# Weight low parts ahead of the output weight's, ten small products in four groups, and the low rank's rows in another bank

## The reference, cut to what matters

```python
x = x + L0_xattn(layernorm(x), ctx, mask, position_bias, ...)   # 32 heads of 128
x = x + L0_ffn(layernorm(x), W_base, lora_A, lora_B, router_W, router_b, prior, active)
x = x + L1_xattn(layernorm(x), ctx, Wq, bq, Wk, bk)             # one head of 512
x = x + L1_ffn(layernorm(x), dequantised 6-bit weights, bias)
```

```python
y = einsum('bth,oh->bto', x, W_base) + b_base
A, Bm = lora_A[active], lora_B[active]
z = einsum('bth,erh->bter', x, A)
contribs = einsum('bter,eor->bteo', z, Bm) * 2.0
logits = (einsum('bth,eh->bte', x, router_W) + router_b)[..., active]
alpha = softmax(log(prior[active] + 1e-12) + logits)
return y + einsum('bteo,bte->bto', contribs, alpha)
```

## Time and profile before

| | |
|---|---|
| median of 3 runs | 953.75 us (952.48 to 953.95) |
| the profiled execution | 953.5 us, of which the span is 951.6 us |
| mean granted TensorE clock | 0.996 of full |
| PE busy | 935.6 us, 98% of the span |
| PE weight loads busy | 816.3 us, 86% |
| DVE busy | 633.0 us, 67% |
| ACT busy | 409.0 us, 43% |
| POOL busy | 522.7 us, 55% |

### The profile page before, as it was taken

How to read it: one execution, slowest core, us unless ns; L and a number is a source line. 1 busy time by engine, 2 the same in 40 slices (tenths; PEclk the granted TensorE clock), 3 DMA queues, 4 the chain that set the end, 5 groups by cost and what they waited for, 6 DMA issues and landing times.

```text
span 951.6 us, 16937 instructions
## 1 busy us (share of the span) xinstructions
PE 935.6 (98%) x5509; PEld 816.3 (86%) x5509; DVE 633.0 (67%) x1158; ACT 409.0 (43%) x1141; POOL 522.7 (55%) x583
## 2 busy tenths in 40 slices
PE   9999999999999999999999999999999999999996
PEld 8888898888889888888888888888888887877774
DVE  5675764565756676657675667567666768767876
ACT  5654535334344434443433343434343444335563
POOL 3450734476556756575657475746575654032567
PEclk9999999999999999999999999999999999999999
DMA  9224437563668466736573657456763764300001
GB/s 331 106 78 149 133 133 279 204 237 133 231 227 285 149 227 225 273 116 256 200 275 131 234 205 280 174 178 246 264 203 128 272 222 145 137 24 1 34 23 67
DMA packets 61146, 171.70 MB, mean 180 GB/s; under 512 B 6039, under 2 KB 8219, under 8 KB 60844
## 3 DMA queue, kind: packets, MB, share of 16 engines
q1 hardware_dynamic: 61100, 171.11, 50.8%
HBM read 159.56 MB, written 11.53 MB: 180 GB/s over the span
## 4 chain that ended last, share of the span: by engine, by line
PE 92%; DVE 2%; ACT 1%; POOL 1%; issue 1%; DMA 1%; SPq 0%; POOLq 0%; ACTq 0%; DVEq 0%
PE ps_q L353 7%; PE ps_q L355 7%; PE ps_q L354 7%; PE ps_o L353 6%; PE ps_o L355 6%; PE ps_o L354 6%; PE ps_k L353 6%; PE ps_t L2132 6%; PE ps_k L355 6%; PE ps_k L354 6%; PE ps_v L353 6%; PE ps_s L2105 6%; PE ps_v L355 6%; PE ps_v L354 6%; PE ps_t L2122 3%
## 5 line engine op out<-in xcount | busy, mean ns | idle before, releaser
L767 ACT ACTIVATE scores<-scores,neg_max 128x128 f32<-128x128 f32 x256 | 100.1, 393 | 219.1 <-DVE neg_max L1549 219.0
L1436 DVE TENSOR_TENSOR acc<-ps_o,acc 128x512 f32<-128x512 f32 x128 | 87.9, 687 | 65.9 <-PE ps_o L355 65.9
L353 PE MATMUL ps_o<-wo_hi,att_hi 128*128 128x512 f32 x256 | 106.0, 414 | 0.6 <-issue 0.5
L355 PE MATMUL ps_o<-wo_hi,att_lo 128*128 128x512 f32 x256 | 100.5, 393 | 0.0
L354 PE MATMUL ps_o<-wo_lo,att_hi 128*128 128x512 f32 x256 | 100.2, 391 | 0.0
L773 ACT COPY probs_t<-ps_t 128x512 f32<-128x512 f32 x64 | 37.7, 589 | 140.4 <-PE ps_t L2122 140.4
L1076 POOL TENSOR_TENSOR shift<-bias_sb,mask_sb 128x512 f32<-128x512 f32 x64 | 84.2, 1316 | 2.9 <-DVE scores L1545 2.9
L1424 DVE TENSOR_TENSOR att_lo<-ps_t,att_hi 128x512 fp32r<-128x512 f32 x64 | 44.2, 691 | 55.2 <-ACT att_hi L760 55.1
L1117 POOL TENSOR_TENSOR wq_lo<-raw_q,wq_hi 128x256 fp32r<-128x256 f32 x65 | 48.0, 739 | 59.0 <-ACT wq_hi L599 59.0
L353 PE MATMUL ps_v<-wv_hi,ct_hi 128*128 128x256 f32 x264 | 75.0, 284 | 0.1
L355 PE MATMUL ps_v<-wv_hi,ct_lo 128*128 128x256 f32 x264 | 74.7, 283 | 0.0
(11 more groups left out here) (378 smaller groups left out, 2785.1 us busy)
## 6 DMA issues: line engine op xcount, KB each, us to landing
ring_hi<-scratch_x_t SPq DMA_DIRECT2D x39, 512.0 KB, 4.0
ring_lo<-scratch_x_t SPq DMA_DIRECT2D x39, 512.0 KB, 4.9
ring_hi<-scratch_c_t SPq DMA_DIRECT2D x39, 512.0 KB, 4.1
ring_lo<-scratch_c_t SPq DMA_DIRECT2D x39, 512.0 KB, 5.3
raw_o<-in_w_o SPq DMA_DIRECT2D x16, 512.0 KB, 4.7
raw_q<-in_w_q SPq DMA_DIRECT2D x15, 512.0 KB, 6.1
raw_k<-in_w_k SPq DMA_DIRECT2D x15, 512.0 KB, 6.9
xt_hi<-scratch_x_t SPq DMA_DIRECT2D x13, 512.0 KB, 7.3
```

The lines of the kernel that those rows point to most:

```text
L353: pe.matmul(dst, hi_l, hi_r, start=first, stop=False)
L355: return pe.matmul(dst, lo_l, hi_r, start=False, stop=last)
L767: e = act.activation(probs[n][:, m, :], scores[n][:, m, :], ACT.Exp, bias=neg_max[:, n, m:m + 1], accum_out=row_sum[:, n, m:m + 1])
L1436: dve.tensor_tensor(acc[:, b, :], ps_o[:], acc[:, b, :], ALU.add).then_inc(o_added, 1)
```

## The change

It has four parts. Nothing that is computed is changed.

1. Steps 60 and 61. ACT makes the third high part of Wk ahead of the evacuation of the transposed probabilities and the fourth ahead of `split_o`. POOL makes three low parts of Wk, then the output weight's low part, then the fourth of Wk. PE runs `k_p3` ahead of the output product of step 60 instead of behind it.
2. The ten small products, which were one group behind `product_g(0)`, become four groups: a pair behind each of `product_g(0)`, the second part of the output product of step 62, `product_g(1)` and `product_g(2)`; the last group has the two bias products too. DVE's copies of them and ACT's logarithm move back to match.
3. The two products with `lora_B`'s rows move behind `product_g(3)` and write bank `ps_k2` instead of `ps_v`. DVE's three instructions that read them move behind `a_rest(0)` and `g_evac(3)`. As `ps_k2` is also the bank of `product_g(4)`, that product now waits for the last of the three (`lb_out`, 3), and `a_low_rank(0)` waits for the copies of part 2 instead.
4. `r_junk`, into which DVE's `r_batch` writes, lies on the mask's place, since the router's weights are now still in use when the first `r_batch` runs.

```diff
@@ ACT
             wk1_high_part(0)
             wk1_high_part(1)
+            wk1_high_part(2)
             pt_evac(STEPS - 4)
+            wk1_high_part(3)
             split_o(GROUPS - 1)
             attention_high(STEPS - 4)
-            wk1_high_part(2)
-            wk1_high_part(3)
...
-            act.wait_ge(lr_mm, 1)
-            act.activation(logit_bias[:, 0, :], ps_v[:, 148:152], ACT.Ln, bias=prior_eps[:, 0:1]).then_inc(lbias, 1)
             pt_evac(STEPS - 1)
...
             attention_high(STEPS - 1)
+            act.wait_ge(lr_mm, 1)
+            act.activation(logit_bias[:, 0, :], ps_v[:, 148:152], ACT.Ln, bias=prior_eps[:, 0:1]).then_inc(lbias, 1)
@@ POOL
-                if c % 4 == 0:
+                if last and c == 4:
+                    for m in range(NC):
+                        if m == NC - 1:
+                            rest_o(g)
+                        pool.wait_ge(w1_hi_s, m + 1)
+                        pool.tensor_tensor(wk1_lo[:, m, :], wk1_raw[:, m, :], wk1_hi[:, m, :].bitcast(F32),
+                                           ALU.subtract).then_inc(wk1_lo_s, 1)
+                elif c % 4 == 0:
                     rest_o(g)
@@ DVE
             add_output(STEPS - 2, 6, (1,))
-            dve.wait_ge(lr_mm, 1)
-            dve.wait_ge(lbias, 1)
-            dve.tensor_copy(low_rank_in[:], ps_v[:, 0:NC * ZL].rearrange("p (c z) -> p c z", z=ZL)).then_inc(lr_out, 1)
-            dve.wait_ge(lr_out, 1)
-            dve.tensor_tensor(logit_bias[:, 1, :], logit_bias[:, 0, :], ps_v[:, 144:148], ALU.add).then_inc(lr_out, 1)
...
             g_evac(1)
-            dve.wait_ge(lb_mm, 1)
-            dve.tensor_copy(stacked[0:STACK, :], ps_v[0:STACK, :]).then_inc(lb_out, 1)
...
             attention_rest(STEPS - 1)
             r_batch(2)
             r_batch(3)
             g_evac(2)
-            add_output(STEPS - 1, LOOP_STEPS - 1)
+            dve.wait_ge(lr_mm, 1)
+            dve.wait_ge(lbias, 1)
+            dve.tensor_copy(low_rank_in[:], ps_v[:, 0:NC * ZL].rearrange("p (c z) -> p c z", z=ZL)).then_inc(lr_out, 1)
+            dve.wait_ge(lr_out, 1)
+            dve.tensor_tensor(logit_bias[:, 1, :], logit_bias[:, 0, :], ps_v[:, 144:148], ALU.add).then_inc(lr_out, 1)
+            add_output(STEPS - 1, LOOP_STEPS - 1, (0,))
             statistics(0, 1, o_added, ready(1))
             a_rest(0)
             g_evac(3)
+            dve.wait_ge(lb_mm, 1)
+            dve.tensor_copy(stacked[0:STACK, :], ps_k2[0:STACK, :]).then_inc(lb_out, 1)
+            dve.wait_ge(lb_out, 1)
+            dve.tensor_tensor(stacked[2 * RR:STACK, :], ps_k2[2 * RR:STACK, :], stacked[2 * RR:STACK, :].bitcast(F32),
+                              ALU.subtract).then_inc(lb_out, 1)
+            dve.wait_ge(lb_out, 2)
+            dve.tensor_copy(stacked[3 * RR:3 * RR + 1, :], ps_k2[3 * RR:3 * RR + 1, :]).then_inc(lb_out, 1)
+            add_output(STEPS - 1, LOOP_STEPS - 1, (1,))
@@ PE
+                if last and c == 5:
+                    k_p3(g)
                 output(s - 1, (c - 1) % LOOP_STEPS, g if c % 4 == 1 else None, (0,))
...
                 if last and c == 5:
-                    k_p3(g)
                     pe.wait_ge(v_out, v_count(i, 14))
...
                 if n == 4:
                     pe.wait_ge(att_lo_s, STEPS)
                     pe.wait_ge(odd_in, 32 * TURNS - 16)
+                    pe.wait_ge(lb_out, 3)
...
             product_g(0)
+            small_pair(0)
+            output(s - 1, 6, None, (1,))
+            small_pair(1)
+            step_transpose(s, 7)
+            product_g(1)
+            small_pair(2)
+            step_values(s, 7, v_count(TURNS - 1, 14))
+            product_g(2)
+            small_pair(3)
             for n in range(2):
                 last = pe.matmul(ps_v[:, NC * ZL + ACTIVE * n:NC * ZL + ACTIVE * (n + 1)], rb_cols[:, n, :],
                                  select[0:EXPERTS, STACK:SL], start=True, stop=True)
             last.then_inc(lr_mm, 1)
             output(s, 7, None, (0,))
             product_g(3)
+            pe.wait_ge(vec_in, 48)
+            pe.matmul(ps_k2[0:STACK, :], select[:, 0:STACK], lora_b_sb[:], start=True, stop=False)
+            pe.matmul(ps_k2[0:STACK, :], bias_pick[:], b_row[:], start=False, stop=True).then_inc(lb_mm, 1)
             output(s, 7, None, (1,))
...
             def a_low_rank(b):
                 if b == 0:
                     pe.wait_ge(g_out, 2)
-                    pe.wait_ge(lb_out, 3)
+                    pe.wait_ge(lr_out, 2)
```

More of the change, by code:

```diff
@@ L120, in build @@
         bias_sb, _ = place("bias_sb", [P, 2, 2, P], F32)
-        mask_sb, _ = place("mask_sb", [P, BATCH, P], F32)
+        mask_sb, at_mask = place("mask_sb", [P, BATCH, P], F32)
         ident, _ = place("ident", [P, P], F32)
@@ L213, in build @@
         rb_cols, _ = place("rb_cols", [EXPERTS, 2, P], F32, at=at_qkv[0] + 8192 + 3072)
-        r_junk, _ = place("r_junk", [P, D], F32, at=at_qkv[0] + 8192)
+        r_junk, _ = place("r_junk", [P, D], F32, at=at_mask)
         r_diag = [place(f"r_diag{n}", [P, P], F32, at=at_qkv[0] + 8192 + 2048 + 512 * n)[0] for n in range(2)]
@@ L1240, in step @@
                     rest_v(PLAIN)
[L1241 to L1245, removed]
                 if c == 1 and own:
@@ L2509, in _, with small_pair @@
             spread_kb()
[L2511 to L2515, removed]
+            def small_pair(c):
+                if c == 0:
+                    pe.wait_ge(sel_s, 1)
+                    pe.wait_ge(rbc_s, 2)
+                    pe.wait_ge(lora_in, 48)
                 cols = slice(c * P, (c + 1) * P)
@@ L2519, in _ @@
                           start=True, stop=True)
+            product_g(0)
+            small_pair(0)
[7 more added lines that the diff above has]
+            small_pair(3)
             for n in range(2):
```

## The result

The changed kernel takes 958.26 us in the median of 6 runs (957.01 to 958.85), the one before 953.66 (6 runs, 952.48 to 953.95). The ratio is 1.0045 with a 95% interval of 1.0034 to 1.0056: slower, by 4.6 us. The profiled execution took 958.27 us with a span of 956.5, against 951.6 before. Two executions of the later sessions, one of the kernel before and one of the kernel with POOL's waits, took some 1554 us at a mean granted clock of 0.56 and are left out of every comparison.

A forecast was written before the change was run, and what follows sets the result against it. PE's stream of matmuls was taken to bound the kernel (92% of the chain). -0.8 (step 61) - 1.4 (small products) + 4.85 (idle) + 1.7 (clock) = +4.35 us on 953.75: 958.1 us, range 955.6 to 960.0.

The forecast's parts named there:

- Step 61: In step 61, DVE's last softmax instruction ends earlier under the new POOL order: gain 0.8 us, bounds 0 and 2.1.
- `neg_max`'s coin flip: In step 61, neg_max comes within 0.1 us of a border between POOL instructions: slips through or waits until 799.7.
- Small products: Behind the ten small products, four groups keep the clock up: gain 1.7, less 0.3, net 1.4 us; bounds 0 and 1.9.
- The chain: Last stages' start: batch 0's transposition, through ACT and DVE, releases product_g(4) after 5.20 us; PE idles 4.85, bounds 4.6 and 5.1.
- The clock after it: Behind the idle stretch at product_g(4), the clock falls and costs PE 1.7 us; bounds 0 and 2.7.
- Nothing taken back: After product_g(4), in the last stages, nothing takes back the 4.85 us of idle time.
- A: At product_g(4), the idle stretch is there but the clock behind it costs nothing: 956.4 us; chance 0.18.
- B: At product_g(4), something overlooked releases it in time and only the gains stay: 951.55 us; chance 0.05.
- D: Gains in step 61 and small products at upper bounds (2.1, 1.9), no clock cost after the idle: 954.6 us; chance 0.03.
- C: The clock still falls once, among the four groups of small products or in step 61: 959.8 us; chance 0.12.

The follow-up runs named there:

- POOL waits: The reads first kernel plus two POOL waits, for DVE's neg_max and last softmax instruction of step 61; 950.5 us, 0.9966 of before.
- the rows alone: The kernel before with only part 3 of the change (lora_B's products into ps_k2, DVE's reads late); 960.15 us, 1.0066 of before.
- filled: The changed kernel with 19 unread wide products on PE between the transposition of batch 0 and product_g(4); 955.69 us, 1.0016 of before.
- the reads first: The changed kernel with DVE's three reads of ps_k2 ahead of a_rest(0) and g_evac(3); 951.34 us, 0.9979 of before.
- the other bank: The changed kernel with product_g(4) in ps_v instead of ps_k2, the wait for DVE's reads moved to a_end(0); 952.64 us, 0.9988 of before.
- step 61 alone: The kernel before with only part 1 of the change (new order in steps 60 and 61); 952.35 us, 0.9981 of before.
- one group again: The reads first kernel with the ten small products back in one group behind product_g(0); 953.37 us, 0.9991 of before.
- without step 61: The reads first kernel with part 1 (steps 60 and 61) undone; 952.68 us, 0.9993 of before.
- rows earlier: The POOL waits kernel with lora_B's two products ahead of product_g(3) instead of behind it; 949.55 us, 0.9959 of before.

## Why the prediction was right, point by point

- **Forecast and result.** 958.1 us was forecast as the likeliest, 958.26 measured; the change in the profiled execution was to be +4.35 and is +4.77, of which 0.50 lies ahead of the change. That the number is so close is in part luck. Between the scores of step 61 and `a_low_rank(0)` the terms were to be -0.8, -1.4, +4.85 and +1.7, and came as -1.29, -1.58, +4.95 and +2.29: gains 0.67 us larger and costs 0.69 us larger than forecast, which cancel.
- **Step 61.** -0.8 was forecast, -0.96 came by the transposition, and -0.33 more between it and the small products, where PE had waited for DVE twice by 0.1 to 0.2 us (for the last part of `wq_lo` and for `w_rows`). The mechanism is shown by the run in which POOL waits: the small DVE instructions end when the POOL instruction that is under way ends. Two details were otherwise than forecast. In the new order it was the factor ahead of the multiplication that waited for the second shift; the multiplication itself took 0.69 us, against 1.72 before, and that is the gain. And before, the multiplication did not end with POOL's instruction, as the prediction's sentence on the trace has it, but ran on for 0.56 us behind it. The term was too small by 0.49 us, 0.33 of them since I followed the saving no further than the transposition. The rule of the Trainium skill that the prediction cites for the two engines' shared port pair ("SBUF — State Buffer") held: `neg_max` took 1.27 us beside a POOL instruction and 0.17 without.
- **`neg_max`'s coin flip.** I left open whether it slips in between two POOL instructions. In all traces of the new order it didn't: 1.27 us. With POOL held off it took 0.17.
- **Small products.** -1.4 was forecast net, -1.58 came between these two executions. Its two halves were both off: the fall of the clock was to be worth 1.7 us and is worth 1.57 (20.39 or so with it, 18.82 without, one group in both), and the 0.3 us for three more places where wide products follow small ones didn't come (18.79 or 18.80 with four groups against 18.82 with one). Besides, as a mean over runs the step was mis-sized: I read one fall of the clock in one execution as a fall in each. Of 59 runs of the kernel before in the sessions of the experiments, 19 had a mean clock of 0.998 or more and took 952.6 us in the mean, 28 had 0.996 to 0.997 and took 954.2, and 12 had less and took 955.4. If the falls of these runs lie behind the small products, as the one in the profiled execution does, the gain of the four groups is 1.6 us in some two runs out of three, and nothing in the third; where the clock fell in runs without a trace isn't shown. The profiled execution, 953.5 us, was one of those with a fall.
- **The chain.** 5.20 us from the transposition to `product_g(4)` were forecast, 5.30 came in the changed kernel, in the rows alone and in the filled one. Each link is where the prediction had it. The 0.10 lies between DVE's last read and PE (0.15 us and not 0.05). That the chain starts on PE itself is shown by two runs: the reads first, and the other bank.
- **The clock after it.** 1.7 us was forecast, 2.29 measured, inside the bounds of 0 and 2.7. Of the low clock, 1.8 us (852.3 to 854.1) lay in idle time and cost nothing, but it lasted 6.8 us in all (to about 859.1), twice as long as behind the small products, where I had taken the price from. That PE pays for it is shown by the filled run (2.3 us less at `product_g(4)` with 19 products more). The rule of the Trainium skill about waits that put TensorE back to half clock ("TensorE: Matmul & The Clock Gate") held: idle for 4.70 us, clock at 0.50.
- **Nothing taken back.** From `a_low_rank(0)` to the last matmul the two traces differ by 0.01 us. Waits later in the pipeline (0.24, 0.44, 0.31 us and so on) are the same in both; I take it that each is counted from PE's own earlier work.
- **Rivals.** A, B and D would have needed a smaller clock term, an early read or larger gains; none came. C's fall of the clock among the four groups didn't come in any trace of them.

## What to carry to other kernels

When a buffer is given a second use, ask what stands ahead of its last read in the reader's queue, and whether any of it waits for the engine that wants the buffer back. If it does, the reads can't be early, however idle the reader is: here DVE sat idle for 6.2 us (844.3 to 850.5) ahead of them, for the last 3.2 of these with the reads' data there (PE had written them by 847.4), and their move ahead of what they stood behind was worth 6.9 us. TensorE's idle stretch of some 5 us cost half as much again through the clock here, and a gain read from one fall of the clock has to be looked for in several runs before it is counted in full.

## What the runs showed that I had not expected

- The same group of ten small products, at the same place and with the same neighbours ahead of it, brings the clock to 0.50 in some executions and not in others: 0.66 over 5 us in three traces (before, step 61 alone, one group again), 1.00 in a fourth (the rows alone), and mean clocks of 0.992 to 0.999 among 12 runs of one kernel. What decides it isn't settled by these runs. One such fall, 3.4 us at half clock, takes 0.002 off the mean clock of an execution, so runs at 0.994 or 0.992 have more low clock than that, in places that no trace shows. I only saw that with the products in four groups, 40 of 41 runs without a new idle stretch had a mean clock of 0.998 or more (the reads first 9 of 9, without step 61 10 of 11, filled 11 of 11, POOL waits 5 of 5, rows earlier 5 of 5). The kernel with the other bank has them in four groups as well, but 6 of its 11 runs are at 0.996; where their clock was low is open. The profiled one, at 0.999, has its wait of 1.44 us with the clock at 1.00 around it. So that four groups keep the clock up is likely, and not shown for every kernel that has them.
- Filler products were no loss in this idle stretch: 19 wide products of 0.23 us whose results nobody reads made the kernel 2.6 us faster.
